# Rejoining, statistics and transposes moved to the head of the group in the projection stage of a fused two-layer model

## The reference

```python
# end of the mixture of experts: two experts' rows per token, weighted
x = x + w[:, 0] * y0 + w[:, 1] * y1
# the mix: the block's own layer norm over the outer one
z = layernorm(x)
h = layernorm(z) * ln1_w + ln1_b
q, k, v = h @ q_w.T + q_b, h @ k_w.T + k_b, h @ v_w.T + v_b
q, k = elu(q) + 1, elu(k) + 1        # as max(q, 0) + exp(min(q, 0))
```

## Time and profile before

| | us |
|---|---|
| median of 3 executions | 4011.05 |
| lowest, highest | 4006.26, 4012.92 |
| the profiled execution, its own time | 4012.92 |
| its span in the profile | 4010.8 |
| TensorE busy | 3263.8 (81%) |
| VectorE busy | 2661.1 (66%) |
| ScalarE busy | 1690.6 (42%) |
| POOL busy | 1378.5 (34%) |

### The profile page before, as it was taken

How to read it: one execution, slowest core, us unless ns; L and a number is a source line. 1 busy time by engine, 2 the same in 40 slices (tenths; PEclk the granted TensorE clock), 3 DMA queues, 4 the chain that set the end, 5 groups by cost and what they waited for, 6 DMA issues and landing times. The chain is left out here.

```text
span 4010.8 us, 55646 instructions
## 1 busy us (share of the span) xinstructions
PE 3263.8 (81%) x16440; PEld 1860.8 (46%) x16441; DVE 2661.1 (66%) x5097; ACT 1690.6 (42%) x3279; POOL 1378.5 (34%) x1379
## 2 busy tenths in 40 slices
PE   4877787788658979889897989977787778898885
PEld 1333333233225654444444436655456456566464
DVE  2999899899976757575674847687534866223435
ACT  3655545555515535556365555411222333222222
POOL 2777777677730020110202000053454200001453
PEclk8988898899988988979798899988899989999998
DMA  3544545454430000000000000170034588000146
GB/s 89 132 124 122 122 129 124 114 131 129 132 84 1 1 15 1 2 1 2 2 2 2 2 1 1 56 189 0 35 117 133 167 143 98 16 16 0 59 129 201
DMA packets 370275, 283.15 MB, mean 71 GB/s; under 512 B 214026, under 2 KB 290366, under 8 KB 370016
## 3 DMA queue, kind: packets, MB, share of 16 engines
q1 hardware_dynamic: 356960, 246.43, 25.0%
q0 software_dynamic: 13056, 33.65, 2.5%
HBM read 205.69 MB, written 76.16 MB: 70 GB/s over the span
## 5 line engine op out<-in xcount | busy, mean ns | idle before, releaser
L428 POOL TENSOR_TENSOR mamba_dBu<-mamba_du,mamba_bcs 128x512 f32<-128x512 f32 x512 | 642.1, 1269 | 272.1 <-DMA mamba_bcs<-mamba_bc 209.2
L378 PE MATMUL mamba_banks<-mamba_hc,ident 128*128 128x512 f32 x1024 | 553.9, 663 | 216.7 <-DVE mamba_hc L598 154.0
L551 ACT ACTIVATE mamba_banks<-mamba_delta,mamba_a_neg 128x512 f32<-128x512 f32 x512 | 352.3, 691 | 240.1 <-DVE mamba_hc L598 231.0
L1403 DVE TENSOR_REDUCE attn_mp<-attn_banks 128x1 f32<-128x512 f32 (+3 forms) x768 | 382.2, 551 | 96.7 <-PE attn_banks L1126 54.0
L378 PEld LDWEIGHTS mamba_banks<-mamba_hc,ident 128*128 128x128 f32 x1024 | 194.9, 208 | 539.0 <-DVE mamba_hc L598 308.8
L591 DVE TENSOR_TENSOR_SCAN mamba_banks<-mamba_banks,mamba_dBu 128x512 f32<-128x512 f32 x256 | 312.1, 1219 | 93.8 <-POOL mamba_dBu L428 59.0
L598 DVE TENSOR_TENSOR mamba_hc<-mamba_banks,mamba_bcs 128x512 f32<-128x512 f32 x512 | 344.1, 673 | 23.8 <-PE mamba_banks L378 23.6
L591 DVE TENSOR_TENSOR_SCAN mamba_banks<-mamba_banks,mamba_h_end,mamba_dBu 128x512 f32<-128x512 f32 x256 | 327.3, 1279 | 28.2 <-ACT mamba_banks L551 19.8
L1123 PE MATMUL attn_banks<-attn_kT,attn_qT 96*128 96x512 bf16 (+3 forms) x768 | 273.8, 372 | 10.6 <-ACT attn_kT L1292 4.9
L1311 ACT ACTIVATE attn_probs<-attn_banks 128x512 f32<-128x512 f32 (+1 forms) x384 | 182.0, 528 | 180.6 <-PE attn_banks L1142 156.0
L1139 PE MATMUL attn_banks<-attn_qT,attn_kT 98*128 98x512 bf16 (+3 forms) x768 | 248.9, 339 | 10.2 <-ACT attn_probs L1311 5.3
(11 more groups left out here) (374 smaller groups left out, 6568.5 us busy)
## 6 DMA issues: line engine op xcount, KB each, us to landing
mamba_bcs<-mamba_bc SPq DMA_DIRECT2D x256, 512.0 KB, 4.9
moe_slots_moe<-moe_pad SPq DMA_DIRECT2D x2, 9252.0 KB, 53.0
moe_xg<-moe_slots_moe SPq DMA_DIRECT2D x144, 128.5 KB, 2.1
mix_qkv<-mixA_qkv SPq DMA_DIRECT2D x8, 1536.0 KB, 5.9
mixA_y<-moe_rows SPq DMA_DIRECT2D x16, 512.0 KB, 5.8
mix_qk<-mix_qkv SPq DMA_DIRECT2D x16, 512.0 KB, 7.7
mix_v<-mix_qkv SPq DMA_DIRECT2D x16, 256.0 KB, 7.6
mix_out<-mixB_oh SPq DMA_DIRECT2D x16, 256.0 KB, 7.4
```

Source lines behind the costliest of these rows:

```text
L378: pe.matmul(banks[:, SUMS + k % PAIR, :], c.ident[:, :], hc[:, n % RING, :], start=(st == 0), stop=True, skip_group_check=True).then_inc(s ...
L428: pool.tensor_tensor(dBu[:, n % RING, :], du[:, v, k, :], bcs[:, i_of(n) % 4, 0, :], ALU.mult)\
L551: act.activation(banks[:, n % RING, :], delta[:, v, k, :], ACT.Exp, scale=a_neg[:, k, st:st + 1])\
L1403: dve.tensor_reduce(mp[:, qt // GT, j, qt % GT, at // 512:at // 512 + 1], banks[:, item % SLOTS, 0:size], AX.X, ALU.max).then_inc(sem("rin ...
```

## The change

On VectorE the rejoining and the moments of group g + 2 no longer stand between the evictions of group g: they come ahead of all four (`moments` calls `rejoin` itself now). The normalisation of group g + 2 still stands between the second and the third eviction. With them the rejoining comes ahead of the waits for `stored` and `qkv_ready` at the head of `take`. On TensorE the transposes of group g + 1 come ahead of all four tiles of group g. No instruction is added or removed, and the other engines' programs are as before.

```diff
@@ TensorE
-                def group(g, slot, first=False, second=False, ahead=2):
+                def project(g, slot, first=False):
                     pe.wait_ge(norm.xT_ready, g * KD + KD)
                     for j in range(GT):
-                        if j == 2 and ahead >= 1:
-                            norm.transposes(pe, g + 1)
                         if not (first and j < 2):
                             pe.wait_ge(qkv_biased, g * GT + j - 1)
...
+                def group(g, slot, first=False, second=False, ahead=2):
+                    if ahead >= 1:
+                        norm.transposes(pe, g + 1)
+                    project(g, slot, first)
@@ VectorE
-                def moments(g):
+                def moments(g, slot):
+                    rejoin(g, slot)
                     if not (isinstance(g, int) and g == 0):
                         dve.wait_ge(norm.r2_ready, g)
...
                     for j in range(GT):
+                        if j == 2 and ahead >= 2:
+                            normalise(g + 2)
                         dve.wait_ge(qkv_filled, g * GT + j + 1)
                         dve.tensor_tensor(qkv[:, slot, j, :], qp[:, j % 2, 0:3 * D], bias[:, :], ALU.add).then_inc(qkv_biased, 1)
-                        if j == 0 and ahead >= 2:
-                            rejoin(g + 2, slot)
-                        if j == 1 and ahead >= 2:
-                            moments(g + 2)
-                        if j == 2 and ahead >= 2:
-                            normalise(g + 2)
...
                 def group(g, slot, first=False, second=False, ahead=2):
+                    if ahead >= 2:
+                        moments(g + 2, slot)
                     take(g, slot, first, second, ahead)
                     elu(g, slot)
```

More of the change, by code:

```diff
@@ L2477, in normalise @@
                                           norm.rstd[:, j:j + 1], ALU.subtract, ALU.mult).then_inc(norm.z_ready, 1)
-                rejoin(0, 0)
-                moments(0)
+                moments(0, 0)
                 normalise(0)
@@ L2486, in _ @@
                 dve.tensor_tensor(bias[:, :], qp[:, 0, 0:3 * D], b0[:, :], ALU.add).then_inc(bias_ready, 1)
-                rejoin(1, 1)
-                moments(1)
+                moments(1, 1)
                 normalise(1)
```

## The result

The median went from 4011.05 to 4030.49 us (7 runs each); the ratio is 1.0052, with a 95% interval of 1.0043 to 1.0061, so 17 to 24 us slower. The profiled execution took 4033.20 us, its span is 4031.1. I had forecast 4024.8 with an upper end of 4030.0. The direction and the place were right, the size was not.

What follows compares the result with a forecast made beforehand. VectorE was taken to set the stage's pace. Terms 3.3 + 5.6 + 6.2 - 1.4 = 13.7 us on a profiled 4012.92 gave 4026.6; with the median 1.9 lower, the forecast was 4024.8, range 4014 to 4030.

Steps and rivals of the forecast that it cites:

- Steady group, evictions without cover: Five steady groups: third and fourth evictions wait 0.86 and 1.71 us for uncovered tiles; 16.40 us a group, +5.6 us.
- 1.1 of changed spacing: Steady group: an amount in us counted beside the waits gained and lost, to reach +1.11 us a group.
- The clock in these groups: Five steady groups: longer TensorE gaps bring the lower clock, 1.25 us each, +6.2 us, between 0 and 8.5.
- the nine gaps: First stage: TensorE gaps of 4.1 us and more ahead of like matmuls, all nine followed by the lower clock.
- First group: Stage's opening: transposes precede the first tiles, partly at the lower clock; +3.3 us, or +1.1 at full clock.
- Last two groups: Groups 6 and 7: group 6 takes 11.6 us for 12.97, group 7 is unchanged; -1.4 us.
- Other queues: SP's y transfers and the stores: the earlier request for y costs nothing; without cover 0.9 us each for two groups.
- The rival with the clock holding: Steady groups keep the full clock: +7.5 us, or 5.3 with a full-clock first group; 4016 to 4018.6; chance 0.15.
- The faster rival: Steady groups: evictions never wait for tiles, 13.83 us a group; -7.6 us, 4003.4; decided by tiles in time; chance 0.08.
- the third rival: Steady groups and group 6: late y transfers or full spells of low clock; 4028 to 4030; chance 0.10.
- the binding transfers: Part of the third rival: y transfers come late for two groups, up to 1.8 us.
- the full spells: Part of the third rival: low-clock spells cost their full 1.7 us, 8.5 in all, one in group 6 too.

Runs made afterwards that it cites:

- e3_kept_busy: The changed kernel plus 36 transposes into an unused PSUM bank ahead of tile j=2 in groups 1 to 5; ratio to the kernel before 1.0021.
- e5_again: The changed kernel, unchanged, a second time on another chip; ratio to the kernel before 1.0038, stage 154.8 us.
- e4_three_halves: The changed kernel with a third part of PSUM tile qp, so tiles 0, 1 and 2 are computed ahead; ratio to the kernel before 1.0000.
- e9_before_again: The kernel before, unchanged, as its own comparison; ratio 0.9995, stage 134.6 us.
- e6_half_filled: The changed kernel plus 18 transposes into an unused PSUM bank ahead of tile j=2 in groups 1 to 5; ratio to the kernel before 1.0028.

## Why the prediction was wrong in size

- *Steady group, evictions without cover: +5.6.* Right. 16.40 us was worked out, and e3_kept_busy measures 16.40. The last decimal is luck: its first eviction comes 5.31 us into the group (3198.33 to 3203.64) for 5.21, and the next group begins 2.40 us behind the ELU (3212.34 to 3214.74) for 2.50. The waits for POOL and ScalarE are gone. The "1.1 of changed spacing" belongs to no term: 15.29 - 0.65 - 0.8 + 0.86 + 1.71 is 16.41 without it.
- *The clock in these groups: "I take the middle of 0.84 and 1.70, 1.25, five times".* This is the step that failed. Five groups of 16.40 would take 82.0 us, they take 92.7: the clock costs **10.7**, 2.1 a group, above the upper end of 8.5 that I gave. Of the shown groups one lost 1.55 us (3151.41 to 3159.43, 8.02 us for 6.47) and the next 2.81 (3169.37 to 3178.65, 9.28); the other three lost 1.71, 2.95 and 1.70. I had taken the dearest spell of the stage, 1.70, for the dearest there is, and looked only at 2 us behind the nine gaps, where the question was how long the lower clock lasts. That every gap brings it was right. With 10.7 in place of 6.2 the sum is 18.2 us, and the forecast 4029.3. With the gaps filled the clock is 1.00. That bears out a rule of the Trainium skill (Perfetto Trace Analysis, Matmul Optimizations), that matmuls should come back to back in batches.
- *First group: +3.3.* In the pair of profiles it was +1.7. Transposes and tiles stand as forecast, but the transposes began 0.7 us earlier in the stage (20.8 us into it for 21.5), and the lower clock ended in the first tile, so that the first eviction came 5.2 us behind the start of the transposes and not 6.0. Both differ from one execution to the next: in e5_again the transposes begin 21.5 us into the stage (3153.98 to 3175.44), as forecast, the first eviction comes 6.0 us behind them (3181.39), and group 1 begins at 39.8, 3.2 us later than in the first profile of the kernel before. Compared with profiles that open alike, the term is 3.2 us (5.49 us for the first matmuls in both) or 2.6 (38.3 for 35.7, 4.58 and 4.73); so it was nearly right, and that the pair of profiles shows only 1.7 is chance.
- *Last two groups: -1.4.* In the pair of profiles -1.7, but by a spell that the kernel before does not always have. As a property of the change it is 0.
- *Other queues: 0.* Right for this kernel; e4_three_halves shows the cover gone, at 0.93 and 0.39 us, one of the bounds I had given (0.9 each).
- The sum with measured terms is 1.7 + 5.6 + 10.7 - 1.7 = 16.3, the stage's lengthening in the pair of profiles. Against e9_before_again it is 2.6 + 5.6 + 10.7 + 0 = 18.9, and the measured change is 17 to 24 us. The medians differ by 19.4. Between the two profiles the stretch ahead of this stage differs by 1.4 us, the one behind it by 2.6, and in e5_again the changed kernel cost 10 to 21 us. Whether a microsecond or two is lost elsewhere stays open.
- *The rival with the clock holding* is what e3_kept_busy built by hand. *The faster rival* had its point of decision right, tiles in time, and e4_three_halves showed its group of 13.83 us. The Trainium skill (Perfetto Trace Analysis, Identifying the Most-Contended Engine) goes by occupancy, and by that alone one would have chosen it. Of the third rival, *the binding transfers* wait behind it (0.93 and 0.39 us in e4_three_halves), and *the full spells* came nearest of all: it had 8.5 us for the clock, still 2.2 too few.

## What to carry to other kernels

With a PSUM tile of two parts, what stands between the evictions is what hides the matmuls: before moving work out from between them, compare the time from freeing a part to its next result (3.9 us here) with what is left between. Price a gap on TensorE with the clock behind it, and read how long the lower clock lasts rather than how deep it is just behind the gap: here a gap of 5 us cost 1.6 to 3.0 us more behind it. Look at small waits of the fullest engine for work that merely stands ahead in another engine's queue: one exchange there took 5 to 8 us off the stage. And profile the unchanged kernel twice before putting a spell of low clock into a sum: here two such profiles differ by 2.6 us in this stage.

## What the runs showed of the hardware

- Behind gaps of 4.8 to 5.0 us in the changed kernel the granted clock stayed at 0.50 to 0.55 for 3.3 to 3.8 us in three groups and for 5.8 us in two, in the same loop with the same work; behind the gaps of 0.9 to 1.0 us in e3_kept_busy it never fell.
- The length of a gap alone does not tell: in e6_half_filled gaps of 2.87, 2.98 and 2.99 us brought the lower clock and gaps of 2.92 and 2.93 did not; in the kernel before one of 3.24 us did not and one of 1.98 did.
- Transposes alone are enough to hold it: 36 of them, 4.09 us of work in a gap of near 5, kept it at 1.00 in e3_kept_busy.
- At half clock (0.50 over 2 us from 3128.6 in the changed kernel) the eight transposes took 1.94 to 1.97 us for 1.04 to 1.09.
